# One decoder block on one core: four phases become two programs, and the first loads and rows of a part are issued inside the part before it

## Chip, cores and metric

The kernel runs on one core of one Trainium2 chip. The metric is the device time in microseconds (us) of one execution; lower is better. The engines are TensorE (PE, with its weight loads as PEld), VectorE (DVE), ScalarE (ACT), GpSimd (POOL) and SyncE (SP), which here does nothing but issue DMAs. Each engine runs its own instruction list in order and waits on semaphores.

## The reference

One pre-norm decoder block on `x` (8 batches, 512 rows, 256 features) and `ctx_1024` (8, 64, 256), in float32:

```
x = x + attn(layernorm(x))                 # causal, 16 query heads of 16, 4 key/value heads,
                                           # low-rank projections (Wqa, Wqb, Wkva, Wkvb), RoPE
x = x + xattn(layernorm(x), ctx, ctx)      # q, k, v of 16 heads of 64; q and k l2-normalised; no softmax:
                                           #   out = (qn kn^T) v;  y = Q + out @ wo + bo
                                           #   y + gelu(layernorm(y) @ w1 + b1) @ w2 + b2
x = x + ffn(layernorm(x))                  # gelu(x @ ternary(W1)^T + b1) @ ternary(W2)^T + b2
```

## The kernel before

The work is done in four phases, each with its own block of five instruction lists, its own on-chip tensors and its own semaphores. A block ends with a wait of all five engines for each other. What goes from one phase to the next goes through DRAM.

1. **Projections** (`project_phase`, lines 104 to 520). Batches in pairs. DVE takes moments and normalises, PE transposes and multiplies, DVE multiplies by cos and sin (L315, L316), POOL adds (`p_rot`, L366), ACT and DVE split each result into three bf16 parts (L415, L324, L423, L331). SP stores them: per batch one DMA of values (L209) and three for each of two query units and one key unit (L217, L220). The part buffers form a ring of six units: ACT may write unit n of the next pair only when the stores of unit n have landed.
2. **Attention** (`attend_phase`). The work goes by groups of four heads, 32 groups in all. "Rows": PE multiplies queries by keys (L837), DVE takes row maxima (L704, L708). POOL splits the maxima into three bf16 parts (`split`, L731 to L740), PE turns them (L846), ACT copies them (L790), SP moves them beside the queries (L638). "Scores": PE computes the scores again with the maxima in the contraction (L856), ACT takes the exponential (L803), POOL zeroes what the mask hides (`causal`, L723, one for each of four key tiles), PE multiplies by the values (L867). Group 0's rows, then group 1's rows, must be done before group 0's scores; from there rows run two groups ahead. POOL also converts the weights of the later phases piece by piece (`weight`: L2360 load, L2375 and L2378 split): four pieces before the groups start, then one after the first and one after the last `causal` of each group, until the list is done.
3. **Context** (`prepare_phase`). From `ctx_1024` it makes keys and values (PE, L1324 to L1326) and, for each batch, the product of keys, values and `wo` (units M, then N: PE L1374 to L1376, ACT L1179, DVE L1279). Four tiles t of two batches z; each batch has units M(t,z,0..1) and N(t,z,0..3). After the last N of a batch SP stores it (L1081, two DMAs of 1 MB). ACT evicts V units (L1150). SP loads the softmax sums, DVE inverts them, SP stores them as `rden`.
4. **Mixing** (`mix_phase`). Eight rounds, one or more batches in flight. For each batch SP loads the attention output `p_o` and the inverse sums spread over 16 rows each, `p_ol` (L1520, L1521, four DMAs), and `x` (L1525). DVE multiplies and splits them (`prepare_o`: L1800, L1803, L1806); PE multiplies by `Wout` (`attention_rows`, L2135); DVE adds `x` (L1817; POOL has added the bias to `x` before, L1598) and takes moments; POOL computes two reciprocal roots in seven small steps (L1575, L1595); DVE normalises into `z` (`z1`, L1833); PE transposes it (L2141); ACT and DVE scale and split it (L1680, L1681, L1840); then the stage QUERY begins (PE L2120, eight tiles). Round 0 computes QUERY of batch 0, and inside it, behind the seventh of the eight tiles, `attention_rows` of batch 1.

On SP the mixing phase starts `load_o(0)`, `load_x(0)`, eight DMAs of constants, `load_n(0)` (two DMAs of 1 MB, L1529), then `next_o(1)`, which waits until batch 0's `attention_added` on DVE is through.

## Time and profile before

| | us |
|---|---|
| median of 3 runs | 1238.46 (1235.85 to 1239.85) |
| the profiled execution, its own time | 1238.83 |
| its span, first to last instruction | 1237.0 |
| PE busy | 1020.9 (83%) |
| DVE busy | 796.5 (64%) |
| ACT busy | 650.9 (53%) |
| POOL busy | 369.8 (30%) |

The span is what the trace covers; the execution's own time is 1.8 us more. The mean granted TensorE clock was 0.924 of full speed. Busy shares are means over four phases that have different limits, so they say little about the places where one phase hands over to the next. The chain that ended last was followed back by the profile for two steps only.

### The profile page before, as it was taken

To read this page: it belongs to the slowest core of one execution; us is meant where nothing else is said; L and a number is where in the kernel's file an instruction comes from. 1 tells how busy PE (TensorE), PEld (TensorE's weight loads), DVE (VectorE), ACT (ScalarE), POOL (GpSimd) and SP (SyncE) were. 2 spreads that over 40 slices of the span, in tenths; PEclk is the share of its full clock that TensorE was granted. 3 is DMA by queue.
4 is the path that set the end of the run, shared out by engine and by line. 5 is a ranking of instruction groups with operands and counts; after the bars stand their busy time and mean duration, and the time that the engine had idled before them with its cause. 6 is when DMAs were issued, how large, how long until landed. Compare 5 with 4: busy or idle time off the path is not lost. (4 is left out here: it accounts for less than half of the span.)

```text
span 1237.0 us, 23520 instructions
## 1 busy us (share of the span) xinstructions
PE 1020.9 (83%) x7133; PEld 759.9 (61%) x7133; DVE 796.5 (64%) x1737; ACT 650.9 (53%) x1155; POOL 369.8 (30%) x516
## 2 busy tenths in 40 slices
PE   3777268999999974893479999999999999998997
PEld 2444134444444423772357878878788787887986
DVE  4888476777787814863555657666567575667554
ACT  1333226777777764462136565474654647455554
POOL 0333348775434321010412132221323113221110
PEclk9777669999999986896679999999999999999999
DMA  3332365443333104357311112012121011010001
GB/s 93 101 120 88 107 151 150 135 129 110 105 98 96 37 28 139 145 209 269 124 51 69 52 69 69 33 45 59 68 68 68 17 51 68 17 68 1 19 1 35
DMA packets 56596, 103.93 MB, mean 84 GB/s; under 512 B 10256, under 2 KB 36368, under 8 KB 52432
## 3 DMA queue, kind: packets, MB, share of 16 engines
q1 hardware_dynamic: 53056, 95.63, 24.1%
q0 software_dynamic: 1920, 6.03, 1.6%
q10 hardware_dynamic: 1552, 1.39, 0.5%
q8 instruction: 38, 0.62, 0.2%
q14 instruction: 30, 0.25, 0.1%
HBM read 63.05 MB, written 39.58 MB: 83 GB/s over the span
## 5 line engine op out<-in xcount | busy, mean ns | idle before, releaser
L803 ACT ACTIVATE p_probs<-p_psS 128x512 f32<-128x512 f32 (+1 forms) x352 | 179.1, 557 | 69.4 <-ACTq L802 68.6
L704 DVE CUSTOM_DVE_ANT_0 p_psA<-p_psA,p_mask 128x512 f32<-128x512 f32 (+1 forms) x256 | 155.1, 648 | 62.7 <-DVEq L702 59.7
L1851 DVE TENSOR_TENSOR p_hl<-p_h,p_hh 128x512 fp32r<-128x512 f32 x128 | 100.9, 792 | 119.9 <-DVEq L1850 119.1
L837 PE MATMUL p_psA<-p_ks,p_qs 96*128 96x512 bf16 (+3 forms) x512 | 141.0, 311 | 31.9 <-PEq L835 30.7
L1669 ACT ACTIVATE p_h<-p_psG,w_columns 128x512 f32<-128x512 f32 x128 | 88.2, 689 | 128.2 <-ACTq L1668 127.2
L856 PE MATMUL p_psS<-p_qs,p_ks 99*128 99x256 bf16 (+3 forms) x512 | 127.8, 302 | 17.2 <-PEq L881 14.6
L2135 PE MATMUL p_psY<-p_n,p_hh 128*128 128x256 f32 x512 | 108.1, 294 | 7.4 <-PEq L2126 4.7
L723 POOL TENSOR_SCALAR_AFFINE_SELECT p_probs<-p_probs 128x512 f32<-128x512 f32 x128 | 80.4, 635 | 99.1 <-POOLq L722 96.4
L2135 PEld LDWEIGHTS p_psY<-p_n,p_hh 128*128 128x128 f32 x512 | 87.2, 198 | 15.3 <-issue 14.1
L856 PEld LDWEIGHTS p_psS<-p_qs,p_ks 99*128 99x128 bf16 x512 | 43.6, 97 | 73.4 <-issue 54.4
L867 PE MATMUL p_psO<-p_probs,p_v 128*32 128x512 f32 (+3 forms) x1024 | 86.1, 455 | 2.7 <-PEq L863 2.7
L1670 ACT ACTIVATE p_hh<-p_psG,w_columns 128x512 fp32r<-128x512 f32 x128 | 87.5, 684 | 0.0
L837 PEld LDWEIGHTS p_psA<-p_ks,p_qs 96*128 96x128 bf16 x512 | 50.9, 99 | 58.9 <-issue 46.5
L1575 POOL TENSOR_TENSOR p_var<-p_mv,p_eps 128x4 f32<-128x4 f32 x24 | 6.9, 287 | 256.7 <-POOLq L1581 193.4
L1704 ACT ACTIVATE p_hh<-p_h 128x512 fp32r<-128x512 f32 x64 | 40.4, 633 | 74.0 <-ACTq L1702 74.0
L2135 PE MATMUL p_psY<-w_t,p_hh 128*128 128x256 f32 x256 | 65.4, 289 | 15.0 <-PEq L2221 15.0
L2135 PE MATMUL p_psY<-p_n,p_hl 128*128 128x256 f32 x256 | 74.2, 290 | 0.0
L2135 PE MATMUL p_psY<-w_w_hi,p_hh 128*128 128x256 f32 x256 | 72.7, 284 | 1.7 <-PEq L2126 1.7
L2135 PE MATMUL p_psY<-w_w_lo,p_hh 128*128 128x256 f32 x256 | 72.4, 283 | 0.0
L2135 PE MATMUL p_psY<-w_w_hi,p_hl 128*128 128x256 f32 x256 | 72.2, 282 | 0.0
L1693 ACT ACTIVATE p_q<-p_psG 128x512 f32<-128x512 f32 x64 | 38.3, 599 | 62.8 <-ACTq L1691 62.8
L708 DVE TENSOR_REDUCE p_mx<-p_psA 128x2 f32<-128x512 f32 (+1 forms) x96 | 63.3, 688 | 1.9 <-DVEq L702 1.7
(260 smaller groups left out, 2741.7 us busy)
## 6 DMA issues: line engine op xcount, KB each, us to landing
p_n<-n_parts SPq DMA_DIRECT2D x16, 1024.0 KB, 6.8
p_qs<-q_parts SPq DMA_DIRECT2D x192, 64.0 KB, 2.2
o_sums<-p_o SPq DMA_DIRECT2D x32, 256.0 KB, 2.1
n_parts<-p_nh SPq DMA_DIRECT2D x8, 1024.0 KB, 3.9
n_parts<-p_nl SPq DMA_DIRECT2D x8, 1024.0 KB, 6.0
q_parts<-p_part SPq DMA_DIRECT2D x48, 128.0 KB
p_x<-in_x_dram SPq DMA_DIRECT2D x8, 512.0 KB, 4.4
p_o<-o_sums SPq DMA_DIRECT2D x16, 256.0 KB
```

The lines of the kernel that those rows point to most:

```text
L704: nc.vector.tensor_tensor_reduce(out=bank[:, 0:w], in0=bank[:, 0:w], in1=mask[:, S - w:S], scale=1.0, scalar=MASKED, op0=ALU.add, op1=ALU.max,
L708: nc.vector.tensor_reduce(mx[:, h:h + n, i], bank[:, 0:n * w].rearrange("p (r k) -> p r k", r=n), AX_X, ALU.max).then_inc(A_free, 1)
L723: nc.gpsimd.affine_select(square, square, [[0, G], [1, P]], ALU.is_ge, 0.0, base=0, channel_multiplier=-1).then_inc(masked, 1)
L803: nc.scalar.activation(probs[:, g % 2, at:at + n * w], psS[place(s, turn) % SB][:, 0:n * w], ACT.Exp, scale=SCALE).then_inc(exp_done, 1)
L837: last = nc.tensor.matmul(bank[:, z * w:(z + 1) * w], qs[0:SROWS, k, g * G + r0 + z, i * P:(i + 1) * P], ks[0:SROWS, k, g, 0:w], start=Tru ...
L856: last = nc.tensor.matmul(bank[:, z * w:(z + 1) * w], key, qs[0:SROWS + MROWS, k, h, j * P:S], start=True, stop=True)
L867: last = nc.tensor.matmul(psO[32 * r:32 * r + 32, j * P:S], v[:, k, g, j, :], probs[:, g % 2, at:at + w], start=(j == 0), stop=(j == TT - 1))
L1669: nc.scalar.activation(h[:, s, :], psG[s][:, :], ACT.Gelu, bias=bias[:, m:m + 1])
L1670: nc.scalar.activation(hh[:, s, :], psG[s][:, :], ACT.Gelu, bias=bias[:, m:m + 1]).then_inc(h_ready, 1)
L1704: nc.scalar.activation(hh[:, s, :], h[:, s, :], ACT.Copy).then_inc(qh_dve, 1)
L1851: nc.vector.tensor_tensor(hl[:, s, :], h[:, s, :], hh[:, s, :].bitcast(F32), ALU.subtract).then_inc(h_parts, 1)
L2135: last = nc.tensor.matmul(dst, xx[:, toks], ww[:, k, :], start=(k == 0 and t % 2 == 0 and i == 0), stop=(last_k and t % 2 == 1 and i == le ...
```

## The change

Phases 1 and 2 become one block, and phases 3 and 4 another. Every phase function now returns five functions, one for each engine; the first part's function of an engine is called at the head of the second part's (`front`), and takes a table of pieces of the second part (`behind`) that it runs at named places. The barrier between phases 2 and 3 stays. The on-chip tensors are laid out in another order, so that those which are written early lie where the first part has nothing live. Two other places: the masks of the attention are built at the start of the projections, and a semaphore `released`, which SP gives when all stores of the projections have landed, now holds back POOL's first weight conversions and ACT's first exponentials.

```diff
@@ project: SP @@
-            def stores(b, k):
+            def stores(b, k, ahead=None):
...
+                    if ahead is not None:
+                        ahead(n)
             for k in range(2):
                 load(k, k)
+            behind["constants"]()
...
             for k in range(2):
-                stores(B - 4 + k, k)
+                stores(B - 4 + k, k, behind["first batch"])
...
+            sp.sem_inc(released, 2)
@@ project: DVE, PE @@
             nc.vector.memset(minus_half[:, :], -0.5)
+            behind["constants"]()
...
             low_part(1)
+            behind["masks"]()
             with dve.Fori(0, B // 2 - 1):
...
             pair(False)
+            pe.wait_ge(V_free, 1)
+            pe.sem_inc(V_free, -1)
+            behind["rows"]()
             pe.wait_ge(XR_free, 2)
@@ attend @@
+            def first_batch(n):
+                if n < KVH:
+                    load_queries(0, 0, n)
+                else:
+                    load_keys(sp, 0, 0, n - KVH)
+                    load_values(sp, 0, 0, n - KVH)
+            front({"constants": constants, "first batch": first_batch})
             maxima(0, 0)
...
             weight, pieces = weight_splitter(nc, pool, stage, *split_sems, splits)
...
-            weights(EARLY)
             split(0)
+            pool.wait_ge(released, 1)
+            pool.sem_inc(released, -1)
             weights(EARLY)
             split(1)
+            weights(EARLY)
...
-            for k in range(2):
-                for z in range(2):
-                    load_keys(act, k, k, z)
-                    load_values(act, k, k, z)
+            front({})
+            for z in range(2):
+                load_keys(act, 1, 1, z)
+                load_values(act, 1, 1, z)
...
             maxima(psS[0], 0)
+            act.wait_ge(released, 1)
+            act.sem_inc(released, -1)
             batch(True, True)
@@ prepare: SP @@
             for t in range(NTILE):
                 for z in range(BT):
+                    if (t, z) == (NTILE - 2, BT - 1):
+                        sp.wait_ge(context_free, 1)
+                        sp.sem_inc(context_free, -1)
+                        behind["context"]()
                     sp.wait_ge(n_ready, 1)
...
-            sp.wait_ge(rden_out, 16)
-            sp.sem_inc(rden_out, -16)
+                if t == NTILE - 3:
+                    sp.wait_ge(rden_out, 16)
+                    sp.sem_inc(rden_out, -16)
+                    behind["sums"]()
             for z in range(BT):
                 sp.wait_ge(n_out[z], 32)
                 sp.sem_inc(n_out[z], -32)
@@ prepare: ACT (after V(3,1)), then after each unit on ACT, DVE, PE @@
+                    if (t, i) == (NTILE - 1, 1):
+                        act.drain().then_inc(context_free, 1)
...
+                if u in behind:
+                    behind[u]()
@@ mix @@
+        DIVIDE_AT, O_HIGH_AT, O_LOW_AT = (("N", 2, 0, 0), ("N", 2, 0, 2)), ("N", 2, 1, 0), ("N", 2, 1, 2)
+        ATTENTION_AT, ROWS_AT, Z_AT = ("M", 3, 0, 1), ("N", 3, 0, 1), ("N", 3, 1, 0)
+        TRANSPOSES_AT = ("N", 3, 1, 1), ("N", 3, 1, 3)
+        FEATURES_AT = ((("N", 3, 1, 2), 0), (("N", 3, 1, 3), 1))
...
+            front({"sums": lambda: load_o(0), "context": constants})
             load_n(0)
             next_o(1)
...
+            front({at: lambda c=c: affine(fh, w["ln1_g"], w["ln1_b"], c) for at, c in FEATURES_AT})
...
+            def first_rows():
...
+                dve.sem_inc(out_done, 16)
+                attention_added(True)
+
+            front({DIVIDE_AT[0]: lambda: divide(0), DIVIDE_AT[1]: lambda: divide(1), O_HIGH_AT: o_high, O_LOW_AT: o_low,
+                   ROWS_AT: first_rows, Z_AT: z1})
...
+            def first_transposes():
+                pe.wait_ge(const_in, 16 * 3)
+                z_first()
+
+            front({ATTENTION_AT: first_rows, TRANSPOSES_AT[0]: first_transposes, TRANSPOSES_AT[1]: z_second})
```

(`constants` of the mixing part is `load_x(0)` and the eight DMAs of constants.)

**Place one: SP at the end of the projections.** Before, with the stores of batches 4 to 7 behind each other and the first loads of the attention after them (`p_qs` are queries, `p_ks` keys):

```order
L209 DMA v_ones<-p_v 128x512
L217 DMA q_parts<-p_part 8x16x512 x6
L220 DMA k_parts<-p_part 4x16x512 x3
L108 UNCONDITIONAL_BRANCH
L623 UNCONDITIONAL_BRANCH
L626 DMA p_ident<-in_ident_dram 128x128
L626 DMA p_mask<-in_mask_dram 128x128
L632 DMA p_qs<-q_parts 16x2048 x24
```

Now, in the stores of batches 4 and 5:

```order
L220 DMA q_parts<-p_part 8x16x512 x3
L641 DMA p_qs<-q_parts 16x2048 x6
L223 DMA k_parts<-p_part 4x16x512 x3
L641 DMA p_qs<-q_parts 16x2048 x6
L212 DMA v_ones<-p_v 128x512
L220 DMA q_parts<-p_part 8x16x512 x3
L641 DMA p_qs<-q_parts 16x2048 x6
L220 DMA q_parts<-p_part 8x16x512 x3
L624 DMA p_ks<-k_parts 16x1024 x6
L629 DMA p_v<-v_ones 128x256
L223 DMA k_parts<-p_part 4x16x512 x3
```

Six groups of loads, 38 DMAs, stand between the stores of batches 4 and 5; none stands after the last store.

**Place two: POOL at the start of the attention.** Before, from the second split of maxima backwards, two weight pieces lie ahead of it and none between it and the first `causal` (`p_stage` is the buffer of a weight piece):

```order
L2375 CAST c_wk_hi<-p_stage 128x512
L2378 TENSOR_TENSOR c_wk_lo<-p_stage,c_wk_hi 128x512
L731 CAST p_msplit<-p_mx 128x16
L734 TENSOR_TENSOR p_mrem<-p_mx,p_msplit 128x16
L737 CAST p_msplit<-p_mrem 128x16
L740 TENSOR_TENSOR p_msplit<-p_mrem,p_msplit 128x16
L723 ISA
L723 AFFINE_SELECT p_probs<-p_probs 128x4x128
```

Now:

```order
L755 TENSOR_TENSOR p_msplit<-p_mrem,p_msplit 128x16
L2450 DMA p_stage<-in_L_xattn_wk_dram 128x512
L2465 CAST c_wk_hi<-p_stage 128x512
L2468 TENSOR_TENSOR c_wk_lo<-p_stage,c_wk_hi 128x512
L2450 DMA p_stage<-in_L_xattn_wk_dram 128x512
L2465 CAST c_wk_hi<-p_stage 128x512
L2468 TENSOR_TENSOR c_wk_lo<-p_stage,c_wk_hi 128x512
L738 ISA
L738 AFFINE_SELECT p_probs<-p_probs 128x4x128
```

Two pieces have moved from ahead of the second split to behind it, in front of the first `causal`.

**Place three: SP and DVE at the end of the context part.** On SP, now (before, the rows of `p_o`, `p_ol`, `p_xin` and the constants stood behind the last `n_parts` store and a branch):

```order
L1108 DMA n_parts<-p_nl 128x2048
L1563 DMA p_o<-o_sums 128x1x512
L1564 DMA p_ol<-rden 128x1x512
L1563 DMA p_o<-o_sums 128x1x512
L1564 DMA p_ol<-rden 128x1x512
L1108 DMA n_parts<-p_nh 128x2048
L1108 DMA n_parts<-p_nl 128x2048
L1568 DMA p_xin<-in_x_dram 128x4x256
```

and at its end, where batch 1's loads still come after the last stores and the two loads of `p_n`:

```order
L1108 DMA n_parts<-p_nl 128x2048
L1572 DMA p_n<-n_parts 128x2048 x2
L1563 DMA p_o<-o_sums 128x1x512
L1564 DMA p_ol<-rden 128x1x512
L1563 DMA p_o<-o_sums 128x1x512
```

On DVE, now, the units of tile 2 with the four operations of `prepare_o` between the evictions of N (`p_nl`); before, the evictions stood as `x4` and `x2`, and `p_o<-p_o,p_ol` came behind the last of them:

```order
L1309 TENSOR_TENSOR p_nl<-p_psMN,p_nh 128x512
L1840 TENSOR_TENSOR p_o<-p_o,p_ol 128x512
L1309 TENSOR_TENSOR p_nl<-p_psMN,p_nh 128x512 x2
L1840 TENSOR_TENSOR p_o<-p_o,p_ol 128x512
L1309 TENSOR_TENSOR p_nl<-p_psMN,p_nh 128x512
```

The first of them waits for the four loads that SP issues behind the stores of tile 1.

## Rows read from the trace of the kernel before

**Rows 1.** Busy time by stretch: start:end, length, then each engine's busy us, clock, DMA.

```profile
150.00:175.00 25.00, 10.72 (x38) 4.24 (x39) 14.76 (x35) 0.27 (x1) 8.96 (x15) 0.50 0.82 183
575.00:600.00 25.00, 4.57 (x24) 4.39 (x24) 6.94 (x17) 0.00 (x0) 3.20 (x3) 0.57 0.60 186
```

**Rows 2.** Timeline, projections to first scores: start, us, operation, idle before it.

```profile
140.17 0.68 DVE L331 TENSOR_TENSOR p_part<-p_rem,p_part 64x512 bf16<-64x512 f32 x1 [0.29 <-DVEq L330]
...
160.57 0.70 DVE L704 CUSTOM_DVE_ANT_0 p_psA<-p_psA,p_mask 128x512 f32<-128x512 f32 x1 [2.29 <-DVEq L702]
...
170.29 2.05 PE L837 MATMUL p_psA<-p_ks,p_qs 96*128 96x512 bf16 x5 [0.84 <-PEq L835]
...
176.30 0.63 PE L856 MATMUL p_psS<-p_qs,p_ks 99*128 99x512 bf16 x1
```

**Rows 3.** Timeline of SP, stores of batches 4 to 7 and the first loads.

```profile
105.36 6.68 SPq L217 DMA_DIRECT2D q_parts<-p_part  x6
...
143.66 2.02 SPq L220 DMA_DIRECT2D k_parts<-p_part  x3
...
150.92 9.27 SPq L632 DMA_DIRECT2D p_qs<-q_parts  x20
```

**Rows 4.** Timeline of ACT, the last pair of the projections: its wait for a ring slot.

```profile
136.70 0.63 ACT L415 ACTIVATE p_part<-p_rot 64x512 bf16<-64x512 f32 x1 [0.66 <-ACTq L414]
```

**Rows 5.** Timeline of POOL and PE, first groups of the attention.

```profile
169.36 0.56 POOL L2360 DMA_DIRECT2D p_stage<-in_L_xattn_wk_dram  x1 [0.34 <-issue]
...
173.95 1.26 POOL L2378 TENSOR_TENSOR c_wk_lo<-p_stage,c_wk_hi 128x512 fp32r<-128x512 f32 x1 [0.18 <-POOLq L2377]
...
179.90 0.64 POOL L723 TENSOR_SCALAR_AFFINE_SELECT p_probs<-p_probs 128x512 f32<-128x512 f32 x1 [0.83 <-POOLq L2368]
...
183.10 1.80 POOL L723 TENSOR_SCALAR_AFFINE_SELECT p_probs<-p_probs 128x512 f32<-128x512 f32 x3
...
185.29 1.71 PE L867 MATMUL p_psO<-p_probs,p_v 128*32 128x512 f32 x16
```

**Rows 6.** Timeline of SP from the stores of tile 1 to batch 1's loads.

```profile
538.73 0.43 SPq L1081 DMA_DIRECT2D n_parts<-p_nl  x1
...
569.49 0.33 SPq L1081 DMA_DIRECT2D n_parts<-p_nh  x1
...
576.30 0.72 SPq L1520 DMA_DIRECT2D p_o<-o_sums  x1
...
597.50 0.62 SPq L1520 DMA_DIRECT2D p_o<-o_sums  x1
```

**Rows 7.** Timeline of DVE and ACT, end of context and start of mixing.

```profile
542.37 1.29 DVE L1279 TENSOR_TENSOR p_nl<-p_psMN,p_nh 128x512 fp32r<-128x512 f32 x2 [1.61 <-DVEq L1277]
...
552.35 0.60 ACT L1150 ACTIVATE p_v<-p_psKV 128x512 f32<-128x512 f32 x1 [0.81 <-ACTq L1149]
...
566.53 2.84 DVE L1279 TENSOR_TENSOR p_nl<-p_psMN,p_nh 128x512 fp32r<-128x512 f32 x4 [1.05 <-DVEq L1277]
...
586.99 1.53 DVE L1800 TENSOR_TENSOR p_o<-p_o,p_ol 128x512 f32<-128x512 f32 x2 [9.97 <-DVEq L1799]
```

**Rows 8.** Timeline of PE: attention rows of batch 0, first query tile, attention rows of batch 1.

```profile
591.20 0.55 PE L2135 MATMUL p_psY<-w_wout_hi,p_oh 128*128 128x256 f32 x1 [23.39 <-PEq L2126]
...
611.93 0.77 PE L2120 MATMUL p_psG<-p_fh,w_wq_hi 128*128 128x512 f32 x1 [2.56 <-PEq L2158]
...
624.71 0.28 PE L2135 MATMUL p_psY<-w_wout_hi,p_oh 128*128 128x256 f32 x1
```

**Rows 9.** DMA issues, whole run: tensors, queue, count, KB each, median us to landing.

```profile
p_n<-n_parts SPq DMA_DIRECT2D x16, 1024.0 KB, 6.8
...
n_parts<-p_nl SPq DMA_DIRECT2D x8, 1024.0 KB, 6.0
```

**Rows 10.** The same view, 576 to 590 us.

```profile
p_n<-n_parts SPq DMA_DIRECT2D x2, 1024.0 KB, 10.3
...
p_xin<-in_x_dram SPq DMA_DIRECT2D x1, 512.0 KB, 9.1
```

More of the change, by code:

```diff
@@ L188, in project_phase, with sync @@
         v_out = [sem(f"v_out{k}") for k in range(2)]
-        block = ctx.enter_context(nc.Block())
-        @block.sync
-        def _(sp):
+        released = sem("released")
+        def sync(sp, behind):
             sp.wait_ge(zeroed, 2)
@@ L349, in _, with gpsimd @@
             pair(False)
-        @block.gpsimd
-        def _(pool):
+        def gpsimd(pool, behind):
             def rsqrt(k):
@@ L374, in _, with scalar @@
             pair(False)
-        @block.scalar
-        def _(act):
+        def scalar(act, behind):
             for n in range(RING):
@@ L434, in _, with tensor @@
             pair(False)
-        @block.tensor
-        def _(pe):
+        def tensor(pe, behind):
             pe.wait_ge(weights_pe, 1)
@@ L533, in sem @@
         def sem(name):
-            return ctx.enter_context(nc.semaphore("p2_" + name))
+            return sems.enter_context(nc.semaphore("p2_" + name))
         AHEAD = 2
         NG = G * TT
+        widths = [S - P * j for j in range(TT)]
+        starts = [G * sum(widths[:j]) for j in range(TT)]
+        probs = sb("probs", [P, 2, G * sum(widths)], F32)
+        o = sb("o", [P, 2, S], F32)
         ident = sb("ident", [P, P], F32)
@@ L553, in attend_phase @@
         mrows = sb("mrows", [MROWS * NG, KVH, P], BF16)
-        widths = [S - P * j for j in range(TT)]
-        starts = [G * sum(widths[:j]) for j in range(TT)]
-        probs = sb("probs", [P, 2, G * sum(widths)], F32)
-        o = sb("o", [P, 2, S], F32)
         stage = [sb(f"stage{i}", [P, SPLIT], F32) for i in range(2)]
@@ L669, in batch @@
                         load_queries(1, 1, g + 1)
-            for g in range(KVH):
-                load_queries(0, 0, g)
+            def first_batch(n):
[5 more added lines that the diff above has]
+            front({"constants": constants, "first batch": first_batch})
             maxima(0, 0)
@@ L709, in maxima @@
                                                 ALU.max).then_inc(A_free, 1)
+            front({"constants": constants, "masks": masks})
             with dve.Fori(0, B):
@@ L909, in batch @@
                 return KVH * RING - (0 if has_next else 1) - used[0]
-            for unit in range(len(AUNITS)):
-                score_rows(0, 0, unit)
+            def first_rows():
+                pe.wait_ge(consts_pe, 1)
+                pe.sem_inc(consts_pe, -1)
+                pe.sem_inc(A_free, 4)
+                for unit in range(len(AUNITS)):
+                    score_rows(0, 0, unit)
+            front({"rows": first_rows})
             maxima(psS[0], 0)
@@ L1420, in place, with four_rows @@
             return (stage.first + m) % LAG
+        def four_rows(name):
+            return sb(name, [P, TT, E], F32)
+        xin = four_rows("xin")
+        biases = sb("biases", [P, 4, E], F32)
+        x1, z = four_rows("x1"), four_rows("z")
+        feat = sb("feat", [P, C, S], F32)
+        fh, fl = sb("fh", [P, C, S], F32R), sb("fl", [P, C, S], F32R)
+        q0 = four_rows("q0")
+        oh = sb("oh", [P, C, S], F32R)
+        o = sb("o", [P, C, S], F32)
+        ol = sb("ol", [P, C, S], F32R)
         ident = sb("ident", [P, P], F32)
@@ L1777, in last_round @@
                     gelu(w["fb1"], place(TERNARY_7, m), m)
-            act.wait_ge(act_go, 1)
-            act.sem_inc(act_go, -1)
-            for c in range(C):
-                affine(fh, w["ln1_g"], w["ln1_b"], c)
+            front({at: lambda c=c: affine(fh, w["ln1_g"], w["ln1_b"], c) for at, c in FEATURES_AT})
             round_0()
```

234 lines of the change are left out of this document (119 added, 115 removed).

## The prediction

> **What bounds the kernel now.** I read the busy time by stretch first, since the change touches only the places where one phase hands over to the next. Most stretches are full; two are not. From 150 to 175 us PE is busy for 10.7 of 25 us, at half the clock, and ACT for 0.3; from 575 to 600 PE is busy for 4.6 and ACT not at all [rows 1]. Then the timelines of the engines through both places. At the first, the last operation of the projections on DVE ends at 140.85 us and its next real work, the first row maximum, starts at 160.57; PE's first scores start at 176.30 [rows 2]. In between SP issues its last stores until 145.68, waits for them, and starts on the first queries at 150.92 [rows 3]. At the second, the last eviction of the context part ends at 569.37 [rows 7], SP issues the last store, waits for it to land and starts batch 0's loads at 576.30 [rows 6]; DVE has stood 9.97 us when they arrive at 586.99 [rows 7], PE 23.39 us when its attention rows start at 591.20, and the first query tile starts at 611.93 [rows 8]. So each place is a chain of waits with no engine as its bound, and what is taken out of it comes off the end time, as long as nothing else is late instead.
>
> **First seam, what goes.** The rows of group 0 stand right behind the projections on PE, and DVE's list goes from its last subtraction straight to the first maximum. If queries, keys and masks are there, that maximum starts at 140.9 instead of 160.57, and everything behind it moves by 19.7 us.
>
> **First seam, who has to be in time.** SP issues 38 more DMAs between its stores. Twenty such loads took 9.27 us, 0.46 each [rows 3], so 38 take 17.6 us. I walked SP's list: unit 0 of batch 4 is stored from 105.36 as before, each store takes 0.65, and a load group 2.8 to 3.2. The keys that group 0 needs are issued by 129.9, the last load by 135.0, the last store ends at 147.3 instead of 145.68. Group 0's data have 11 us to land before 140.9: hidden. The store of the ring's last unit, issued until 131.7, must have landed when ACT rewrites it at 136.70 [rows 4]; no row gives its landing, the nearest is 6.0 us for a store eight times its size [rows 9], so 0 to 1 us; I take 0. `released` comes at about 151.5: the last store ends at 147.3, and before the change SP needed some 4.4 us from there until it went on, shortly ahead of 150.92 [rows 3]. POOL's first two pieces wait for it and are done by 157; SP's move of the maxima is issued behind it, is needed at 156.6, and has 5 us. Both fit. The masks fall into a wait of DVE at the start of the projections. Cost 0.
>
> **First seam, what comes back.** POOL is the engine that loses. Two weight pieces have moved behind the second split. In the trace the two took from 169.36 to 175.21, 5.85 us, and POOL then stood idle; the first `causal` ran at 179.90 with only 0.83 us of idle before it [rows 5]. Moved by 19.7 that is 160.2; now the pieces are ahead of it, and it starts at 165.5, 5.3 us late. The second `causal` follows 3.2 us later, with one more piece between (179.90 to 183.10 [rows 5]), and ends at 169.4. PE wants to multiply by the values at 165.6 (185.29 moved [rows 5]) and to use the second tile at 166.4: it waits 3 us there, on `masked`. Behind that instruction the next groups' rows and scores are queued, so DVE and ACT wait too. POOL has nearly no idle time while pieces last, so the rest of its 5.3 us mostly shows later. Between 3.0 and 5.3; I take 4.5, nearer the upper one. First seam: 19.7 - 4.5 = **15.2 us gained** (bounds 13.4 and 16.7).
>
> **Second seam, what goes.** Barrier and landing of the last store, batch 0's loads, and the whole chain from the division to the transposes, which now lies between units of tiles 2 and 3. From last eviction to first query tile it was 611.93 - 569.37 = 42.6 us [rows 7, 8]; now some 2.3 (the last affine pass and its subtraction).
>
> **Second seam, what it costs inside the context part.** In order:
> - The four loads of `p_o` and `p_ol` are issued behind the 2 MB store of tile 1, which SP issues until 539.2 [rows 6], so from 539.2 to 541.7. DVE reaches the first multiplication at 543.0, after half of the row at 542.37 [rows 7]. The only measured arrival is 10.7 us after the first issue (576.30 to 586.99 [rows 6, 7]), in company of `x`; here a 2 MB store is ahead. I take 551, so DVE stands 8 us and evicts nothing; of this PE and ACT make good some 0.5. +7.5 (bounds 2, if they land as soon as issued, and 10).
> - The copy and the subtraction of `prepare_o` in tile 2: +1.3.
> - The attention rows on PE ahead of N(3,0): the 24 matmuls took 4.57 us [rows 1], of which 0.5 fits in a wait: +4.0.
> - `first_rows` on DVE ahead of N(3,0,2): two additions and moments, about half of the 6.94 us that DVE was busy in that stretch [rows 1]: +3.5.
> - `x` and the biases are issued only when V(3,1) is evicted, at 552.35 [rows 7] plus 8, and `x` took 9.1 us [rows 10], and then POOL must add the bias: DVE waits +1.
> - `z1`, the transposes and one affine pass ahead of the last eviction: +2.
> - PE now stands more often inside the part, and the stretches with idle PE show a clock of 0.50 and 0.57 [rows 1]: +2 as an estimate.
>
> Sum 21.3: the last eviction ends at 590.7, the first query tile starts at 593, **19 us** sooner than 611.93.
>
> **Second seam, what comes back.** Batch 1's loads have not moved ahead of anything. SP reaches `next_o(1)` only after the last store has landed (6.0 us [rows 9]) and after `load_n(0)`. With the last eviction at 590.7 the store has landed at 597, `p_n` is issued until 598.7, `p_o` and `p_ol` until 601.2, and by the 10.7 us above they arrive near 610. Before, they were issued at 597.50, 14.4 us ahead of the first query tile [rows 6, 8], and nobody waited. PE wants batch 1's attention rows behind the seventh query tile, 12.8 us after the first (611.93 to 624.71 [rows 8]), that is at 606. DVE's preparation takes 4.2 (586.99 to 591.20 [rows 7, 8]), so they start at 614.2: PE stands 8 us, and the eighth query tile and all norms are queued behind. Against 624.71 the gain is 10.5; less 0.5 for a lower clock behind the wait, **10 us** (bounds 5 and 19).
>
> **A rule weighed.** The two loads of `p_n` that stood behind ten others landed after 10.3 us, against a median of 6.8 [rows 9, 10]; so loads of one queue do hold each other up. The Trainium skill (DMA: Bandwidth & Descriptors, Queues, rings and completion order) says that each DMA engine consumes the descriptors of a queue in ring order. By that rule batch 1's loads get nothing until the 2 MB of `p_n` ahead of them are through, and the time is that of my sum; if they shared the engines freely and landed 7 us after issue, batch 1 would wait 4 us less and the sum would be 1209.5.
>
> **Sum.** 15.2 + 10 = 25.2 us. The profiled execution took 1238.83 us; the median of the runs is 1238.46, 0.4 less. 1238.83 - 25.2 = 1213.6; I say **1213.5 us**.
>
> **Rivals.**
> - *Nothing comes back* (chance 0.20). POOL's lateness is caught up by waits further on and both load groups land in time. For it: ACT and PE wait here and there in the first groups. Gain 17 to 19.7 and 16 to 19: 1200 to 1206.
> - *The second seam nets little* (0.20). Loads of `p_o` land at 553 or later, SP's constants delay the store of batch 5 and ACT's wait for `n_out`, batch 1's loads come at 615. Second seam 0 to 5, first 13 to 15: 1219 to 1226.
> - *The change doesn't do what it says* (0.05): DVE's first maximum isn't sooner, because a wait for queries or `consts_pe` takes the barrier's place; only the second seam counts: 1226 to 1235. Against it: 11 us of cover.
> - *Slower* (0.05, of which 0.02 beyond 0.3%). SP's loads hold up its stores. The part ring then stops ACT, DVE and PE in the last pair. SP is late by 1.6 us with 0.46 us a load; every 0.1 us more on each of 38 makes it 3.8 later and moves the end of the projections by about that. The gain of 25 us is gone at 0.46 + 0.67 = 1.1 us a load, and 1.2 gives 1243. Only DMAs that stall the queue would cost that; the stores in rows 3 took 1.1 each where waits for their data are counted in (6.68 for six), without them 0.65.
>
> **How the numbers follow.** My forecast, both seams shorter and both partly given back, has 0.50; its own range is 1206 to 1219. Part of the first rival lies under 1202 and part of the second, with the last two, above 1223: the range 1202 to 1223 leaves out about 2 in 10. A difference under 0.3%, 3.7 us, is what a measurement of this kernel can't tell from no change: faster 0.95, same 0.03, slower 0.02.
>
> **What would show it.** Right: the first maximum at 141 and first scores near 156.6; a wait of PE of about 3 us before the values of group 0 and POOL busy without a gap there; a wait of DVE of 5 to 9 us before the first `p_o` multiplication, in the middle of the N evictions; first query tile some 34 us (15.2 + 19) before 611.93; then PE idle about 8 us ahead of batch 1's attention rows, DVE waiting for `o_in`. Wrong: a long wait of ACT on ring slots at the end of the projections; `p_o` landing before DVE asks; no idle PE between the seventh and eighth query tile; or waits later in the mixing rounds that were not there before.

## The result, and the profile after

The changed kernel takes 1224.53 us (median of 4 runs, 1222.67 to 1225.77), the kernel before 1238.99 us beside it (4 runs, 1235.85 to 1239.85): a ratio of 0.9884, 95% interval 0.9867 to 0.99. It is 14.5 us faster where 25.2 were forecast. The profiled execution took 1223.7 us, span 1221.9 us, mean granted clock 0.927 of full speed; the span is 15.1 us shorter than that of before.

Where on the way do these 15.1 us come from? I read the same instructions in both timelines. First the end of the attention and the start of the context part, on PE (start, duration, operation, idle time before it). Before:

```profile
458.08 3.99 PE L867 MATMUL p_psO<-p_probs,p_v 128*32 128x512 f32 x32 [2.42 <-PEq L863]
...
474.45 0.28 PE L1299 MATMUL p_psMN<-p_ident,p_vecs 32*128 32x32 f32 x1 [12.38 <-PEq L1298]
```

After:

```profile
442.59 4.02 PE L881 MATMUL p_psO<-p_probs,p_v 128*32 128x512 f32 x32 [2.42 <-PEq L877]
...
458.56 0.28 PE L1330 MATMUL p_psMN<-p_ident,p_vecs 32*128 32x32 f32 x1 [11.96 <-PEq L1329]
```

The last products of the attention start 15.5 us sooner, the context part 15.9 us sooner. All of the gain is there before the second seam begins, and the second seam gives nothing: 15.1 - 15.9 = -0.8 us.

The second seam after, on PE: the first query tile, the last of the seventh, batch 1's attention rows, and the first product of the eighth tile.

```profile
577.27 0.77 PE L2159 MATMUL p_psG<-p_fh,w_wq_hi 128*128 128x512 f32 x1 [2.56 <-PEq L2197]
...
590.82 0.40 PE L2159 MATMUL p_psG<-p_fh,w_wq_lo 128*128 128x512 f32 x1
...
607.10 0.55 PE L2174 MATMUL p_psY<-w_wout_hi,p_oh 128*128 128x256 f32 x1 [15.88 <-PEq L2165]
607.45 0.41 PE L2174 MATMUL p_psY<-w_wout_hi,p_ol 128*128 128x256 f32 x1
...
612.35 0.63 PE L2159 MATMUL p_psG<-p_fh,w_wq_hi 128*128 128x512 f32 x1
```

The first query tile [rows 8] comes 34.7 us sooner. Without the 15.9 us of the first seam that is 18.8 us, as forecast. Then PE stands idle for 15.88 us, where 8 were forecast, and batch 1's rows start 17.6 us sooner than before, 1.7 more than the first seam alone gives. They take 5.25 us (607.10 to 612.35); before the change they took 2.80 [rows 8], until the eighth tile went on:

```profile
627.51 0.39 PE L2120 MATMUL p_psG<-p_fh,w_wq_hi 128*128 128x512 f32 x1
```

The busy time by stretch has the clock in its last column but two, first of the changed kernel, then of the kernel before: 0.50 of full speed against 1.00, that is 1.2 and 2.4 GHz. PE had stood still for 15.88 us ahead of the first.

```profile
607.00:612.00 5.00, 4.91 (x23) 4.94 (x24) 0.00 (x0) 0.00 (x0) 2.02 (x1) 0.50 0.00 0
```

```profile
625.00:628.00 3.00, 3.00 (x26) 2.91 (x26) 0.18 (x1) 1.09 (x2) 0.00 (x0) 1.00 0.00 0
```

So 1.7 - 2.45 = -0.8 us is left, which is the whole of the second seam.

What PE waited for stands on SP and DVE. SP, after (the last store, then batch 1's loads behind `p_n`):

```profile
576.02 0.43 SPq L1108 DMA_DIRECT2D n_parts<-p_nl  x1
...
584.09 0.81 SPq L1572 DMA_DIRECT2D p_n<-n_parts  x2
585.02 0.62 SPq L1563 DMA_DIRECT2D p_o<-o_sums  x1
```

DVE, after: first the wait inside tile 2 that was forecast, then batch 1's preparation.

```profile
536.09 0.69 DVE L1840 TENSOR_TENSOR p_o<-p_o,p_ol 128x512 f32<-128x512 f32 x1 [8.57 <-DVEq L1839]
...
574.85 0.69 DVE L1309 TENSOR_TENSOR p_nl<-p_psMN,p_nh 128x512 fp32r<-128x512 f32 x1 [1.44 <-DVEq L1307]
...
599.24 1.53 DVE L1840 TENSOR_TENSOR p_o<-p_o,p_ol 128x512 f32<-128x512 f32 x2 [20.82 <-DVEq L1839]
600.91 2.60 DVE L1843 CAST p_oh<-p_o 128x1024 fp32r<-128x1024 f32 x1
603.66 3.13 DVE L1846 TENSOR_TENSOR p_ol<-p_o,p_oh 128x1024 fp32r<-128x1024 f32 x1
```

The loads were there 14.2 us after the first of them was issued (585.02 to 599.24). Then the cast and the subtraction took 2.60 and 3.13 us; for batch 0 they took 0.69 and 1.23 before the change. POOL tells why: it was idle until 600.55, and then added biases right beside them.

```profile
600.55 2.42 POOL L1642 TENSOR_TENSOR p_xin<-p_xin,p_biases 128x1024 f32<-128x1024 f32 x1 [33.62 <-POOLq L1664]
602.93 2.78 POOL L1642 TENSOR_TENSOR p_q<-p_q,p_biases 128x1024 f32<-128x1024 f32 x1
```

The first seam after, on DVE (the last operation of the projections, the first maximum), PE (first scores, the wait for values), POOL (the wait for `released`, first `causal`) and SP (last store, first move of maxima):

```profile
142.76 0.68 DVE L340 TENSOR_TENSOR p_part<-p_rem,p_part 64x512 bf16<-64x512 f32 x1 [0.30 <-DVEq L339]
...
143.37 0.68 DVE L719 CUSTOM_DVE_ANT_0 p_psA<-p_psA,p_mask 128x512 f32<-128x512 f32 x1
...
149.87 1.91 SPq L223 DMA_DIRECT2D k_parts<-p_part  x3
...
157.49 0.84 SPq L647 DMA_DIRECT2D p_qs<-p_mrows  x1
...
157.60 0.78 POOL L2450 DMA_DIRECT2D p_stage<-in_selectors_dram  x1 [6.22 <-POOLq L778]
...
161.73 0.58 PE L870 MATMUL p_psS<-p_qs,p_ks 99*128 99x512 bf16 x1 [2.87 <-PEq L910]
...
169.91 0.63 POOL L738 TENSOR_SCALAR_AFFINE_SELECT p_probs<-p_probs 128x512 f32<-128x512 f32 x1
...
174.37 0.85 PE L881 MATMUL p_psO<-p_probs,p_v 128*32 128x384 f32 x8 [1.85 <-PEq L877]
```

The first maximum stands right behind the projections and is 17.2 us sooner [rows 2]. Then the gain shrinks: first scores 14.6 us sooner, first `causal` 10.0 [rows 2, 5].

POOL's splits of maxima make a ruler for the rest of the attention: there are 32, one per group of heads. The times here are the starts of their second step, read off POOL's timeline, and the last column is the distance:

```
split   before   after   sooner by
  1     167.68  150.40   17.28
  2     178.09  162.69   15.40
  3     185.23  175.73    9.50
  6     213.30  202.75   10.55
  7     224.41  211.56   12.85
 13     278.00  264.30   13.70
 32     441.76  427.78   13.98
```

What is lost up to the third split partly comes back at the seventh. The step from 14.0 us at the last split to 15.5 at the last products is no gain of the change: in the last 20 us of the attention the kernel before had a granted clock of 0.83, the changed one 0.91 over the same 111 matmuls. (From the last split to the context part it takes 32.7 us before the change and 30.8 after; in the eleven other kernels below with the merged first part, where this stretch has the same code, it takes 30.2 to 32.6.)

```profile
442.00:462.00 20.00, 14.94 (x111) 5.03 (x110) 0.00 (x0) 11.36 (x23) 5.49 (x10) 0.83 0.08 28
```

```profile
428.00:448.00 20.00, 13.53 (x111) 4.84 (x111) 0.00 (x0) 11.96 (x24) 5.49 (x11) 0.91 0.08 28
```

### The profile page after: what moved, and what is told of

It is laid out like the page before. It is cut to its first block and busy times, and to the rows that moved or that the text cites. A ratio compares the mean times of both kernels' runs of the same rounds, so it can differ in the third digit from the quotient of the medians.

```text
span 1221.9 us, 23498 instructions
## 1 busy us (share of the span) xinstructions
PE 1027.8 (84%) x7133; PEld 766.0 (63%) x7133; DVE 796.7 (65%) x1737; ACT 650.7 (53%) x1155; POOL 369.4 (30%) x516
## 5 line engine op out<-in xcount | busy, mean ns | idle before, releaser
L870 PE MATMUL p_psS<-p_qs,p_ks 99*128 99x256 bf16 (+3 forms) x512 | 129.0, 304 | 18.4 <-PEq L895 12.9
L2174 PEld LDWEIGHTS p_psY<-p_n,p_hh 128*128 128x128 f32 x512 | 85.9, 195 | 16.4 <-issue 15.2
L2174 PE MATMUL p_psY<-w_t,p_hh 128*128 128x256 f32 x256 | 65.4, 288 | 15.1 <-PEq L2260 15.1
```

The lines of the kernel that those rows point to most:

```text
L870: last = nc.tensor.matmul(bank[:, z * w:(z + 1) * w], key, qs[0:SROWS + MROWS, k, h, j * P:S], start=True, stop=True)
L2174: last = nc.tensor.matmul(dst, xx[:, toks], ww[:, k, :], start=(k == 0 and t % 2 == 0 and i == 0), stop=(last_k and t % 2 == 1 and i == le ...
```

## The experiments

**My theory** after the comparison: the first seam gives the whole gain; the second shortens the path to the first query tile by 19 us and gives all of it back ahead of batch 1's attention rows, because batch 1's loads still stand behind the last stores and 2 MB of `p_n`, because DVE prepares them beside POOL, and because PE comes back at half the clock. **Rivals:** the second seam is lost inside the context part (the 8.57 us wait of DVE); batch 1's loads are slow by themselves; moving them only moves the wait. Each kernel was run against the kernel before on the same chip; every ratio below is to it. The changed kernel was not run again beside them, so a distance to it is told twice where it matters: as the difference of the medians, and as the difference of the two ratios, which leaves out what differs between chips.

### Each part alone

`first_only` merges projections and attention and keeps the two blocks of context and mixing; `second_only` does the opposite. The end of `first_only`, against the changed kernel (shortened):

```diff
-            prepare = prepare_programs(nc, ctx, a, scr, w, cw)
-        mix = mix_programs(nc, ctx, a, scr, w, out)
+            prepare_phase(nc, a, scr, w, cw)
+        mix_phase(nc, a, scr, w, out)
```

Expected of the first: 

> One part of the change alone: projections and attention in one block; context and mixing in two blocks as before. My theory: the first seam gave all of the gain. In the two traces the last attention product ends 15.5 us sooner (458.08 against 442.59) and the context part starts 15.9 us sooner, while the end is 15.1 us sooner; so this kernel takes 1223 to 1226 us, the same as the changed one within 0.2%. Rival: both seams gave something (the trace of one execution misled by a different clock), then it is 3 us or more slower than the changed kernel, 1228 or above.

Expected of the second: 

> The other part alone: context and mixing in one block, projections and attention in two blocks as before. My theory: the second seam nets between -1 and +1 us, so 1237 to 1240 us. Its trace should show the first query tile some 19 us sooner and then 15 to 16 us of idle PE ahead of batch 1's attention rows. Rival: it gains 3 us or more, 1236 or below.

Measured: `first_only` 1224.53 us, ratio 0.9897 (0.9872 to 0.9923); `second_only` 1239.52 us, ratio 1.0014 (0.9997 to 1.0031). Both lie in the ranges that I gave the theory. The second part alone is worth nothing, and its trace shows the same exchange, on PE:

```profile
597.07 0.77 PE L2140 MATMUL p_psG<-p_fh,w_wq_hi 128*128 128x512 f32 x1 [2.56 <-PEq L2178]
...
624.22 0.55 PE L2155 MATMUL p_psY<-w_wout_hi,p_oh 128*128 128x256 f32 x1 [14.06 <-PEq L2146]
```

The first query tile is 14.9 us sooner [rows 8] in an execution that reached the attention 2.1 us later (first split at 169.75 against 167.68, in code that both kernels share), so 17 us by the distance; and then PE stands for 14.06 us. I had expected 19 and 15 to 16: the exchange is the same, a little smaller on both sides.

### Batch 1's loads sooner

`o_early`:

```diff
+                    if (t, z) == (NTILE - 1, 0):
+                        behind["second"]()
...
-            front({"sums": lambda: load_o(0), "context": constants})
+            front({"sums": lambda: load_o(0), "context": constants, "second": lambda: next_o(1)})
             load_n(0)
-            next_o(1)
```

> The changed kernel, with batch 1's loads of the attention output, the inverse sums and x issued behind the store of the last batch but one of the context part instead of behind the last store and the loads of p_n. My theory: the 15.9 us of PE ahead of batch 1's attention rows are the wait for these loads and for DVE's preparation behind them. The loads are then issued at about 565, land before 580, DVE prepares until 586, and the rows start right behind the seventh tile at 591 at full clock: 16 us sooner, and 2 us more from the clock, 1206 to 1210 us. Rival one: the wait moves to something else that has to be there for the eighth tile and the norms (the bias added by POOL, p_n, the last stores that the loads now hold up): gain under 8 us, 1217 or more. Rival two: the second seam is lost inside the context part and not at batch 1: gain under 2 us.

Measured: 1208.41 us, ratio 0.9765 (0.974 to 0.979), its profiled execution 1205.26. PE goes from the seventh tile to batch 1's rows without a gap: their first product starts at 593.05, at full clock, and the first query tile was at 579.38, 13.7 us ahead. The rows are 14.0 us sooner than in the changed kernel, and the context part had begun 1.8 us later (460.31 against 458.56): 15.8 us. The loads still took 14.3 us (568.00 to 582.32; I had expected them before 580), this time behind the stores of (3,0), and DVE takes as long as ever, beside POOL, but nobody waits:

```profile
582.32 1.53 DVE L1841 TENSOR_TENSOR p_o<-p_o,p_ol 128x512 f32<-128x512 f32 x2 [1.79 <-DVEq L1840]
584.00 2.66 DVE L1844 CAST p_oh<-p_o 128x1024 fp32r<-128x1024 f32 x1
586.80 3.18 DVE L1847 TENSOR_TENSOR p_ol<-p_o,p_oh 128x1024 fp32r<-128x1024 f32 x1
```

The move of five DMAs is worth 16.1 us by the medians and 14.7 by the ratios. The trace gives 15.8, and 2.4 more because the rows run at full clock; the two profiled executions lie 18.4 apart. Why the medians show less isn't shown. Both rivals of this run fall: nothing took the wait's place.

### Is it the place in the queue?

`o_before_n` only turns two steps round, behind the same wait for the last stores:

```diff
-            load_n(0)
             next_o(1)
+            load_n(0)
```

> The changed kernel, with only the order of two steps of SP turned round: batch 1's five loads first, then the two loads of p_n (2 MB), both still behind the landing of the last stores. Theory of queue order: p_o lands 4 to 5 us sooner (after some 9 to 10 us instead of 14.2), all behind it moves by that, 1219.5 to 1221 us; p_n then lands near 598 and is wanted at 621, hidden. Rival: the loads of p_o are slow by themselves (many small packets), whatever stands ahead: under 1.5 us gained, 1223 or more.

Measured: 1220.0 us, ratio 0.9858 (0.9837 to 0.9879). SP and DVE:

```profile
587.15 0.61 SPq L1563 DMA_DIRECT2D p_o<-o_sums  x1
```

```profile
598.21 1.53 DVE L1840 TENSOR_TENSOR p_o<-p_o,p_ol 128x512 f32<-128x512 f32 x2 [16.80 <-DVEq L1839]
```

From the first issue to the first use it is 11.1 us, against 14.2 behind the 2 MB. With the 0.9 us that SP spent on issuing `p_n` first, the queue's order cost 4.1 us between these two traces. The eight kernels that keep `p_n` ahead have 13.3 to 14.5 us from issue to use, so the price is 3.2 to 4.3. The time shows 4.5 us by the medians and 3.2 by the ratios, whose intervals overlap. The other 11 us the loads need with nothing ahead; batch 0's needed 10.7 [rows 6, 7].

### DVE beside POOL

`pool_order` lets POOL add the biases to batch 0's rows while DVE waits:

```diff
             def round_0():
-                rows_in()
                 q0_rows()
+                rows_in()
                 rsqrt_twice()
```

> The changed kernel, with two steps of POOL turned round in round 0: it adds the biases to q0 and to x of batch 0 (which are ready at 578) before it waits for x of batch 1, so that these two passes run while DVE waits for p_o and not while DVE prepares p_o. Theory: DVE's cast and subtraction in batch 1's preparation took 2.60 and 3.13 us instead of 0.69 and 1.23 because POOL worked at the same time; now only one POOL pass of 2.4 us overlaps, the preparation takes 5 to 6 instead of 7.55 us, and 1.5 to 2.5 us are gained: 1222 to 1223 us. Rival: DVE is slow there for another reason: same time as the changed kernel, and a preparation of 7.5 us in the trace.

Measured: 1223.13 us, ratio 0.9891 (0.9862 to 0.992), which by itself can't be told from the changed kernel. The trace can:

```profile
601.70 2.60 DVE L1843 CAST p_oh<-p_o 128x1024 fp32r<-128x1024 f32 x1
604.45 1.23 DVE L1846 TENSOR_TENSOR p_ol<-p_o,p_oh 128x1024 fp32r<-128x1024 f32 x1
```

The one POOL pass that is left still lies beside the cast (2.60 us); the subtraction has nothing beside it and is back at 1.23. From the first multiplication to the rows on PE it is 5.96 us (600.02 to 605.98) instead of 7.86: 1.9 us, as expected.

The starts and ends say more than "beside". That last POOL pass runs from 601.32 to 603.75, and the cast ends at 604.30, 0.55 us behind it. In the changed kernel POOL's passes end at 602.97 and 605.71, the cast 0.54 us behind the first and the subtraction 1.08 behind the second. Each time DVE's operation ends about as long after POOL's pass as it takes alone (0.69 and 1.23). It also goes the other way: in the kernel before, a POOL pass that started at 590.05, inside the subtraction of batch 0 (589.50 to 590.73), took 2.90 us where others take 2.3 to 2.5, and the subtraction kept its 1.23. So in these rows the two don't share; the one that starts later waits for the other's end. That is read from the rows, whose spans on POOL are rough; no run tested it further.

The kernel before had this too, at batch 1, where the query tiles covered it:

```profile
612.99 3.48 DVE L1800 TENSOR_TENSOR p_o<-p_o,p_ol 128x512 f32<-128x512 f32 x2
616.62 2.67 DVE L1803 CAST p_oh<-p_o 128x1024 fp32r<-128x1024 f32 x1
619.43 1.23 DVE L1806 TENSOR_TENSOR p_ol<-p_o,p_oh 128x1024 fp32r<-128x1024 f32 x1
```

```profile
613.26 2.66 POOL L1598 TENSOR_TENSOR p_q<-p_q,p_biases 128x1024 f32<-128x1024 f32 x1 [3.04 <-POOLq L1620]
615.88 2.85 POOL L1598 TENSOR_TENSOR p_x1b<-p_x,p_biases 128x1024 f32<-128x1024 f32 x1
```

### The wait inside tile 2

`sums_early` issues batch 0's four loads behind the stores of (1,0) instead of (1,1):

```diff
+                    if (t, z) == (NTILE - 3, 0):
+                        sp.wait_ge(rden_out, 16)
+                        sp.sem_inc(rden_out, -16)
+                        behind["sums"]()
...
-                if t == NTILE - 3:
-                    sp.wait_ge(rden_out, 16)
-                    sp.sem_inc(rden_out, -16)
-                    behind["sums"]()
```

> The changed kernel, with batch 0's four loads of p_o and p_ol issued one batch sooner, behind the stores of (1,0) instead of (1,1), some 9 us sooner. Theory: the 8.57 us that DVE waits inside tile 2 for these loads go, and so the whole chain to the first query tile comes 7 to 8 us sooner; the last stores too, and with them batch 1's loads: 1216.5 to 1218.5 us. Rival: PE and ACT had hidden part of this wait, or a later wait (x and the biases, z) takes its place: gain of 4 us or less, 1220.5 or more.

Measured: 1215.92 us, ratio 0.9825 (0.9793 to 0.9856), 0.6 us under the range of its theory; 8.6 us under the changed kernel by the medians, 7.3 by the ratios. The context part starts at 458.61 as in the changed kernel (458.56), and the first query tile at 569.37 instead of 577.27: 7.9 us. So this wait is a true cost of the second seam, the +7.5 of the sum. But batch 1's rows start at 597.53, behind 15.07 us of idle PE: the wait at batch 1 follows the last store and stays nearly as long as it was (15.88).

### The first seam: POOL, SP, or both

Four kernels. `maxima_early` issues the first move of maxima ahead of SP's wait for the last stores. `pieces_late` takes the second pair of weight pieces out and lets a fourth batch do them. `queries_only` loads batch 1's queries at the start instead of behind each group. `queries_ahead` is the last two together.

```diff
 # maxima_early, in the projections' SP list
+            behind["first maxima"]()
             for k in range(2):
                 sp.wait_ge(v_out[k], 16)
 # pieces_late, POOL
-        SPLIT_BATCHES = -(-(len(splits) - 2 * EARLY) // (KVH * TT // 2))
+        SPLIT_BATCHES = -(-(len(splits) - EARLY) // (KVH * TT // 2))
...
             split(1)
-            weights(EARLY)
 # queries_only, SP
             load_queries(1, 1, 0)
+            load_queries(1, 1, 1)
...
-                    if first and g + 1 < KVH:
-                        load_queries(1, 1, g + 1)
+                    if first and g == 0:
+                        load_queries(1, 1, 2)
+                        load_queries(1, 1, 3)
```

> The changed kernel, with SP's move of group 0's maxima issued before SP waits for the last stores of the projections to land, not behind. Theory: first scores at about 156.5 instead of 161.73, no wait of PE there; but POOL, which waits for the landing too and has four weight pieces and a split ahead of its first causal (169.91), is what bounds the first groups, so the time stays within 1 us of the changed kernel: 1223.5 to 1225.5. Rival: the late move of the maxima is what cost the first seam; then up to 4 us are gained, 1220.5 to 1222.

> The changed kernel, with the two weight pieces between the second split and the first causal taken out there and done in the fourth batch of the attention instead, where POOL has room. Theory of my prediction: they make POOL late at the first values; now the first causal runs at about 165.7, bound by ACT's exponentials, 4.2 us sooner, and the gain is 2 to 4 us: 1220.5 to 1222.5. Rival: the lateness of POOL was made good anyway, where SP had been the late one (the splits' distance to before grew again from 9.5 to 14.0 us): gain under 1 us.

> The changed kernel, with batch 1's queries of groups 1 to 3 loaded at the start of the attention (six DMAs more behind the first move of maxima, twelve behind the second) instead of six behind each of three later groups, so that SP no longer issues 22 DMAs between two moves of maxima. Theory: in the changed kernel POOL is the late one there, and hides SP (PE waits 0.57 us for the move at 200.4), so alone this gives 0 to 1 us: 1223.5 to 1225. Rival: SP is the bound by itself, then 2.5 us or more are gained, 1222 or less.

> The run before and the run with the two weight pieces later, both at once. Theory: with the pieces gone from the start, POOL was 3 us sooner, but PE then waited 2.77 us at 199.5 for the maxima that SP moved behind 22 DMAs; POOL and SP each hide the other. Both gone, that wait goes and the 3 us last: 1220 to 1222.5 us, and the distance of the splits to the kernel before is 16 us or more from the seventh on, against 12.3 with the pieces alone. Rival: a third engine holds the groups at the same place (no wait of PE for SP, but the splits no sooner): 1223.5 or more.

Measured: `maxima_early` 1224.93 us, 0.9899 (0.9876 to 0.9921); `pieces_late` 1222.75 us, 0.9877 (0.985 to 0.9905); `queries_only` 1221.79 us, 0.9863 (0.9838 to 0.9889); `queries_ahead` 1220.84 us, 0.9847 (0.982 to 0.9873). By times alone none of the four is told from the changed kernel (0.9867 to 0.99): every interval overlaps with its own. I expected 2 to 4 us of `pieces_late`, and that fell: it is 1.8 by the medians and 0.9 by the ratios. In its trace the first `causal` was indeed sooner (166.00) and the wait for values gone, but later PE waited for SP instead (first SP's move, then PE):

```profile
196.20 0.72 SPq L647 DMA_DIRECT2D p_qs<-p_mrows  x1
```

```profile
199.52 0.38 PE L869 MATMUL p_psS<-p_qs,p_ks 99*128 99x512 bf16 x1 [2.77 <-PEq L894]
```

SP had issued 20 DMAs ahead of it (my expectation said 22), from 185.20 to 196.1, since the move before. The kernel before has the same wait, 1.89 us at 211.84; the changed one has 0.57 at 200.39. `maxima_early` has 2.61 at 204.72, though its POOL is as late as that of the changed kernel, so this wait also differs between executions. The distance to the kernel before, by the splits:

```
split    after   pieces_late   queries_only   queries_ahead
  1      17.28      16.46         17.57          16.33
  3       9.50      12.63          9.81          12.56
  7      12.85      12.34         13.10          15.45
 13      13.70      12.23         13.45          14.92
 32      13.98      11.35         13.74          14.56
```

POOL's lateness costs the changed kernel 3.1 us at the third split (4.0 if each trace is counted from its own first split). By the seventh it is made good (12.85 against 12.34), because the kernel before had to wait for SP there; that a late POOL gives SP time at this place is my reading, and `pieces_late` fits it. With the pieces gone, SP's wait comes forward; with both gone 2.6 us are left at the seventh split (15.45, where I had expected 16 or more), and 1.1 us go again at split 15 (15.08 to 13.98), in the fourth batch, which now does the two pieces. At the last split 0.6 us of the 3.1 remain.

`queries_only` shows nothing in the splits, as the theory has it. Its median lies 1.7 us under the theory's range and in that of the rival, but the trace decides for the theory: its profiled execution is 4.7 us shorter than that of the changed kernel, and its context part starts at 458.61 against 458.56. So those 4.7 us all lie in the second part, whose code is the same.

### Together

`both_early` joins `o_early`, `sums_early` and `pool_order`; `combined` adds the four edits of the first seam.

> Both load groups of the mixing part sooner (batch 0's behind the stores of (1,0), batch 1's behind those of (3,0)) and POOL's steps of round 0 turned round. Theory: the two gains are at different places and add up, 16 and 8.5 us, while POOL's order adds 0 to 1, since DVE's preparation of batch 1 is now nearly hidden: 1199 to 1201.5 us. Rival: with tile 2 shorter, batch 1's loads meet the stores, are late again, or p_n is: 1203 or more.

> All of them together, with the first move of maxima ahead of SP's wait for the last stores too. Theory: the gains of the first block (2.5 to 4 us) and of the second (24) add: 1196 to 1199 us. Rival: the first block's gains don't show beside a change of 24 us, 1199.5 or more.

Measured: 1201.2 us, ratio 0.9695 (0.9661 to 0.973), and 1195.36 us, ratio 0.9652 (0.963 to 0.9674), the second a little under the range of its theory. The first agrees with the sum of its parts. Between the two the intervals overlap, and the traces don't give the 5.8 us to the first seam: `combined` starts its context part 1.8 us sooner, and another 4.8 us lie between there and the first query tile, where the code is the same and the granted clock was 0.88 against 0.83. `combined` is the fastest kernel of this study, 42.4 us under the 1237.8 us of the kernel before beside it. The waits of PE in the stretch 575 to 640 us (engine, line, what it waited for, us in total, times, longest), in the changed kernel and in `both_early`:

```profile
PE p_psY L2174 <- PEq L2165: 17.9, 2, 15.9
PE p_psG L2231 <- PEq L2230: 5.3, 1, 5.3
```

```profile
PE p_psG L2232 <- PEq L2231: 5.3, 1, 5.3
PE p_psY L2175 <- PEq L2166: 3.7, 2, 2.0
```

The wait of 15.9 us is gone. The one of 5.3 us stands in the kernel before too.

## Why the prediction was too low

The forecast was 1213.5 us and the range 1202 to 1223; the time fell outside it, 11 us above the forecast. The step that failed is "second seam, what comes back": its mechanism was right, its size was wrong by 10.8 us.

- **First seam, what goes.** Right: the first maximum follows the projections at once. It was 17.2 us sooner and not 19.7 because the projections ended 2.6 us later. `second_only`, whose projections are those of before, ended them 2.6 us later too (its last operation starts at 142.81, before it was 140.17), so this needs no cause in the change.
- **Who has to be in time.** "Both fit" was wrong. The last store ended at 151.8, not 147.3, and `released` came 5.7 us behind it, at 157.5 instead of 151.5. POOL stood 6.22 us, and the first move of maxima was late: PE waited 2.87 us for it. But `maxima_early` gained nothing by taking that away. PE doesn't wait for the first move in its trace, and still the first `causal` comes 27.5 us after the last operation of the projections starts (172.54 - 145.05), against 27.2 in the changed kernel. With four pieces and a split ahead of the first `causal`, POOL is the one that counts.
- **What comes back, -4.5.** The place was right (POOL without a gap, PE waiting 1.85 us for values, 3 forecast), and the size is near: from the first to the last split 3.3 us are lost. What I did not have is the reason that it is no more: at the seventh split SP is late in the kernel before, and 2.3 us come back there. First seam: 15.2 forecast, 14.0 by the splits and 15.9 up to the context part, of which 1.5 are the better clock of one execution.
- **Second seam, inside the context part, 21.3.** Right as a sum and at its largest term. DVE waited 8.57 us (8 forecast); on the time axis of before, with 15.9 added, the last eviction ended at 591.4 (590.7) and the first query tile came at 593.2 (593). `sums_early` shows that the wait was worth 7.9 us.
- **What comes back: this step failed.** The mechanism was the one described, the size was not. Batch 1's loads came late, as described; but 10 us were to remain, and -0.8 did. Four numbers in a row erred to the same side. *Issue:* SP went on 7.6 us after it had issued the last store, and issued `p_o` at 600.9 on the axis of before, 2.2 us behind the forecast 598.7. Of this 1.3 us may be chance: of the nine kernels with this same wait SP went on after 6.3 us in five, and after 7.6 to 7.7 in four, the changed one among them. *Landing:* they "arrive near 610 by the 10.7 us above"; they arrived at 615.1. The 10.7 us were of loads with no `p_n` ahead of them. The rule that the prediction weighed said that the 2 MB go first, and that "the time is that of my sum"; but the price in the sum left them out. `o_before_n` measures 4.1 us for them, of which 0.9 is SP's issue. *Preparation:* 7.9 us from the first multiplication to the rows, not 4.2. Batch 1's own preparation stood in the trace of before at 7.7 us (612.99 to 620.66, shown above), under the cover of the query tiles; I took batch 0's. *Clock:* 2.45 us for rows at half the clock, not 0.5. 2.2 + 2.9 + 3.7 + 1.9 is 10.7 of the 10.8 us that are missing.
- **The rule weighed.** The Trainium skill (DMA: Bandwidth & Descriptors, Queues, rings and completion order) has each DMA engine take a queue's descriptors in ring order. By that rule, `p_o` lands later behind `p_n` than ahead of it; the traces agree: 13.3 to 14.5 us from issue to use behind it in eight kernels, 11.1 ahead of it in one.
- **The rivals.** "The second seam nets little", 0 to 5 us, with batch 1's loads at 615, came nearest: it had a chance of 0.20, and its range of 1219 to 1226 holds the time. The loads did arrive at 615.1. But its other reasons, losses inside the context part, didn't come: that part took what the sum said, and the loads of batch 0 arrived at 552.0 on the axis of before, against 551 in the sum and 553 or later in the rival. "Nothing comes back" fell. So did "the change doesn't do what it says", by the first maximum at 143.37, and "slower": SP issued query loads at 0.47 us each, as assumed.

What stays open: why SP goes on after 6.3 us in some kernels and 7.6 in others, and why executions of the same projections end up to 3 us apart (their last operation on DVE starts between 142.5 and 145.7 in the kernels with the merged first part). So a microsecond in the first seam is read from distances within a trace rather than from its clock times.

## What to carry to other kernels

When a change shortens the way to a point, list every load whose issue did not move with it, and find who uses it first: here five DMAs that were issued 14 us ahead of the first query tile before the change were issued 8 us behind it after, and moving them gave 15 to 16 us. A price must come from an instruction in the same surroundings: the same queue with the same bytes ahead, the same neighbour engine busy, the same clock; work that was hidden before shows its true duration in the old trace, one only has to read the hidden instance and not the exposed one. And two engines that are late near the same place can cover each other: at the seventh split, taking one lateness away gave -0.5 or 0.3 us, taking both away 2.6, though only 0.6 of it was left at the last.

## What the runs showed of the hardware

DVE's cast of 128x1024 took 0.69 us alone and 2.60 to 2.67 us beside a POOL tensor operation, the subtraction 1.23 alone and 3.13 to 3.18; they ended 0.54 to 1.08 us after POOL's pass did. The same 24 matmuls took 2.80 us at full clock and 5.25 after 15.9 us of idle PE. Where batch 1's loads still stood behind the last stores, SP went on 6.3 us after it had issued the last 1 MB store in five kernels and 7.6 to 7.7 in four; I found nothing in the traces that tells these apart. With batch 1's loads issued ahead of that store (`o_early`, `both_early`, `combined`) it took 8.9 to 9.7 us.
